# Gated attention's weighings in two column tiles of 64 queries, and the routers' products in column tiles

## The reference

```python
h = x @ rW1.T + rb1                       # 64 features
h = relu(layernorm(h) * ln_g + ln_b)
logits = h @ rW2.T + rb2                  # 8 experts
tp, ti = top_k(softmax(logits), 2)
...
def expert_step(acc, params):             # for each of the 8 experts
    q, k, v = x @ qw.T + qb_, x @ kw.T + kb_, x @ vw.T + vb_   # split into 16 heads of 8
    p = softmax(einsum('bhqd,bhkd->bhqk', q, k) * scale)
    o = einsum('bhqk,bhkd->bhqd', p, v)
    o = o.reshape(B, S, E) @ ow.T + ob_
    return (acc + o * g[..., None], None)
```

## Time and profile before

| | before |
|---|---|
| median of 3 runs | 3347.18 us |
| profiled execution, span | 3447.8 us |
| TensorE busy | 2817.4 us (82%) |
| VectorE busy | 1989.0 us (58%) |
| ScalarE busy | 1326.8 us (38%) |
| mean granted TensorE clock | 0.896 of full speed |

### The profile page before, as it was taken

One profiled execution on the slowest core, in us unless ns is written; L12 is line 12 of the kernel. 1 busy time (PEld: TensorE's weight loads), 2 busy tenths in 40 slices (PEclk: granted clock), 3 DMA queues, 4 the chain that ended last, 5 costly groups with the idle time before them and its releaser, 6 DMA issues.

```text
span 3447.8 us, 64821 instructions
## 1 busy us (share of the span) xinstructions
PE 2817.4 (82%) x24730; PEld 1996.0 (58%) x24818; DVE 1989.0 (58%) x6643; ACT 1326.8 (38%) x3062; POOL 635.1 (18%) x847
## 2 busy tenths in 40 slices
PE   5788988766687987988988988988988988987953
PEld 2344766634574864764764764755755755656743
DVE  2566444456544455666666666666766766765532
ACT  2343434433474743333333333334334334334521
POOL 0122112322312011121121121121111111111043
PEclk7888999877898998998998999998999999998977
DMA  7300647400373700000000000000000000003454
GB/s 254 113 23 22 199 129 208 131 19 22 125 229 99 240 23 7 3 9 7 3 9 7 3 9 7 3 9 7 3 9 7 3 9 4 3 4 112 130 168 147
DMA packets 146658, 217.14 MB, mean 63 GB/s; under 512 B 20392, under 2 KB 99248, under 8 KB 146224
## 3 DMA queue, kind: packets, MB, share of 16 engines
q1 hardware_dynamic: 134064, 187.80, 17.8%
q0 software_dynamic: 12288, 25.19, 2.4%
HBM read 159.83 MB, written 53.08 MB: 62 GB/s over the span
## 4 chain that ended last, share of the span: by engine, by line
PE 58%; DVE 21%; ACT 10%; issue 5%; another core or an unknown queue 2%; SPq 2%; DMA 1%; POOL 1%; DVEq 0%; POOLq 0%; ACTq 0%
PE bank L447 5%; PE bank L383 5%; ACT ex L1153 5%; PE bank L540 4%; PE bank L622 4%; DVE mx L1615 4%; PE bank L548 4%; PE bank L389 3%; PE bank L604 3%; PE bank L467 3%; PE bank L457 3%; PE bank L451 3%; PE bank L436 3%; PE bank L374 2%; PE bank L430 2%
## 5 line engine op out<-in xcount | busy, mean ns | idle before, releaser
L1153 ACT ACTIVATE ex<-bank 128x512 f32<-128x512 f32 x896 | 472.1, 600 | 692.7 <-PE bank L457 456.7
L1615 DVE TENSOR_REDUCE mx<-bank 128x4 bf16<-128x512 f32 x640 | 407.6, 684 | 133.2 <-PE bank L436 68.9
L965 POOL TENSOR_TENSOR rstd<-vare,power 128x2 f32<-128x2 f32 x192 | 136.1, 709 | 1377.9 <-DVE vare L1406 1377.9
L1032 POOL TENSOR_TENSOR oT<-oT 128x128 f32<-128x128 f32 x256 | 118.3, 462 | 916.2 <-DVE oT L1734 915.6
L540 PE MATMUL bank<-qm,expert 128*128 128x128 f32 x1872 | 260.2, 283 | 16.9 <-DMA expert<-in_moe 9.3
L974 POOL DMA_INDIRECT sent<-tail_tok,pos x192 | 192.0, 1000 | 394.0 <-DVE pos L1543 349.9
L383 PE MATMUL bank<-hT,wproj 128*128 128x256 f32 x736 | 242.8, 426 | 25.2 <-DVE oT L1734 8.5
L1607 DVE RECIPROCAL rden<-bank 128x16 f32<-128x16 f32 x160 | 41.1, 257 | 384.9 <-PE bank L476 347.1
L447 PE MATMUL bank<-qm,kf 32*128 32x512 f32 x1280 | 211.4, 723 | 57.1 <-ACT ex L1153 36.2
L540 PEld LDWEIGHTS bank<-qm,expert 128*128 128x128 f32 x1872 | 237.0, 198 | 28.6 <-DMA expert<-in_moe 15.5
L622 PEld LDWEIGHTS bank<-ev,ex 128*128 128x128 f32 x2048 | 247.6, 193 | 5.2 <-issue 0.4
(11 more groups left out here) (208 smaller groups left out, 5064.8 us busy)
## 6 DMA issues: line engine op xcount, KB each, us to landing
expert<-in_moe SPq DMA_DIRECT2D x78, 578.0 KB
expert<-in_moe SPq DMA_DIRECT2D x78, 512.0 KB
expert<-in_moe SPq DMA_DIRECT2D x78, 384.0 KB
sent<-zeros SPq DMA_DIRECT2D x8, 2560.0 KB, 12.8
ex<-sent SPq DMA_DIRECT2D x234, 64.0 KB
answered<-qm SPq DMA_DIRECT2D x234, 64.0 KB
ctxT<-ctx_kept SPq DMA_DIRECT2D x32, 128.0 KB
wproj<-in_wproj SPq DMA_DIRECT2D x1, 3072.0 KB
```

Of the source, the lines that this page charges most:

```text
L1153: give(nc.scalar.activation(ex[s][:, i], ps[:].rearrange("p (i q) -> p i q", i=4), ACT.Exp, scale=SCALE), *key)
L1615: give(nc.vector.tensor_reduce(mx[s][:, b, HB * i:HB * i + HB], ps[:].rearrange("p (i k) -> p i k", i=HB), AX.X, ALU.max), *k, "s", b, i)
```

## The change

`weigh` of the gated attention loads 64 of a block's 128 queries at a time. The first half's result goes to PSUM partitions 0 to 63, the second half's to 64 to 127, in the same columns of the bank as before. `by_token` gets a width: with `wide` under 128 the tokens are loaded in pieces of that many columns, and each piece's result goes to its own partitions. The routers use 32, the gated router's first product 64; values and outputs keep 128. Two costs that the planner reads are lowered by 0.9. What is read and written, and by which other engine, stays.

```diff
--- before.py
+++ after.py
@@ -383,11 +383,15 @@
                         mm = nc.tensor.matmul(ps[:, n * NT:(n + 1) * NT], W(weight), src[:], start=True, stop=True)
                     filled(mm, *k, what)
 
-                def by_token(k, what, weight, src, n, rows_=P):
+                def by_token(k, what, weight, src, n, rows_=P, wide=P):
+
+
                     ps = open_bank("g", *k, what)
                     for b in range(NB):
-                        mm = nc.tensor.matmul(ps[:, b * n:(b + 1) * n], src[0:rows_, seq(b)], weight,
-                                              start=True, stop=True)
+                        for at in range(0, P, wide):
+                            mm = nc.tensor.matmul(ps[at:at + wide, b * n:(b + 1) * n],
+                                                  src[0:rows_, b * P + at:b * P + at + wide], weight,
+                                                  start=True, stop=True)
                     filled(mm, *k, what)
 
                 def keys_values(k, key, value, rot=False):
@@ -402,7 +406,7 @@
                     if w.new("weights_in", 16 * n_loads):
                         pe.wait_ge(sem["weights_in"], 16 * n_loads)
                     taken(*t, "tT")
-                    by_token(t, "logits", router[:, ROUTERS[tail_layer(t[2])], :], attT[s], NE)
+                    by_token(t, "logits", router[:, ROUTERS[tail_layer(t[2])], :], attT[s], NE, wide=32)
 
                 def ranks(t):
 
@@ -619,16 +623,17 @@
                             ps = open_bank("g", *k, "o", p, b)
                             for c in range(4):
                                 j, i = c // 2, c % 2
-                                mm = nc.tensor.matmul(ps[:, c * (HE + 1):(c + 1) * (HE + 1)],
-                                                      ex[s][:, 2 * (p % 2) + i, 2 * b + j, :], ev[s][:, p % 2, b, i, :],
-                                                      start=True, stop=True)
+                                for part in range(2):
+                                    mm = nc.tensor.matmul(ps[head(part), c * (HE + 1):(c + 1) * (HE + 1)],
+                                                          ex[s][:, 2 * (p % 2) + i, 2 * b + j, head(part)],
+                                                          ev[s][:, p % 2, b, i, :], start=True, stop=True)
                             filled(mm, *k, "o", p, b)
 
                     def turn_mixed(p):
                         pe.wait_ge(sem[f"e_summed{s}"], w.next(f"e_summed{s}", NB))
                         turn(k, mixed[s][:, p % 2], f"mixedT{p}")
 
-                    by_token(k, "r", rw1[:], hT[s], HE)
+                    by_token(k, "r", rw1[:], hT[s], HE, wide=HE)
                     keys(0)
                     yield "router", 0.6, 3.0
                     keys(1)
@@ -639,7 +644,7 @@
                     keys(2)
                     yield "router", 0.6, 0.5
                     taken(*k, "rT")
-                    by_token(k, "logits", rw2[:], rT[s], NE, HE)
+                    by_token(k, "logits", rw2[:], rT[s], NE, HE, wide=32)
                     values(1)
                     yield "gate", 0.5, 4.0
                     pe.wait_ge(sem[f"slots_ready{s}"], w.next(f"slots_ready{s}"))
@@ -666,7 +671,7 @@
                             values(n)
                         if n >= 3:
                             turn_mixed(n - 3)
-                        yield "gated unit", 3.6 if 2 <= n < HP else 2.5 if n <= HP + 1 else 0.3, 0.3 if n <= HP else 1.5
+                        yield "gated unit", 2.7 if 2 <= n < HP else 1.6 if n <= HP + 1 else 0.3, 0.3 if n <= HP else 1.5
                     taken(*k, "wtsT")
                     if w.new("bias_in", 1):
                         pe.wait_ge(sem["bias_in"], 1)
```

## The result

The changed kernel takes 3343.35 us (median of 16 runs) where the kernel before takes 3351.30 on the same chip (16 runs). The ratio is 0.9975, 95% interval 0.9964 to 0.9987: 8 us faster, 4 to 12. I had forecast 59 us. The sign is right, the time lies in the range, and the size is out by a factor of seven.

What follows compares the result with a forecast made beforehand. TensorE was taken to bound the gated pass. Weighings 112.6, routers 15.7 + 5.2 + 3.5, less switches 61, gave 76 us; times 0.8, 61, scaled by 0.971 to 59, so 3288 us, range 3230 to 3365.

Steps and rivals of the forecast that it cites:

- rival C: All 128 weighings: column tiles load in turn, a round takes 0.112 us, switches are pure cost; 3383 us, chance 0.15.
- 68 forecast: All gated weighings: 0.88 us less each, minus 0.35 for switches, nets 0.53 us each, 68 us in all.
- the 0.145 and 0.20 of the forecast: TensorE's changes of tiling around a weighing: 0.145 us going in, 0.20 us coming out.
- 76 was forecast: TensorE work shed in the profiled execution: 112.6 + 15.7 + 5.2 + 3.5 - 61 = 76 us.
- 0.57 us or more on L383: Sign of the switch: the queries' two products before a weighing take 0.57 us or more, not 0.43.
- 54 + 57 = 111 ns: Round of a weighing by the skill's rule that loads overlap products only across row groups; equals the loads-in-turn time.
- How much reaches the end? … I take 0.8: Share of the 76 us of shed TensorE work that shortens the kernel: 0.8, so 61 us, scaled 59.
- 90 to 98% busy: TensorE's busy share in slices with weighings, from which shed work there was expected to shorten the pass.
- rival A: Only the weighing's part on the chain of waits counts: 0.56 x 76 = 43 us, scaled 41; 3306 us, chance 0.23.
- Rival B: Gated pass: TensorE's clock falls to 0.90, its work grows 58 us and gives the gain back; 3344 us, chance 0.10.
- I put the order at nothing, between -15 and +20 us: Planner's costs lowered by 0.9 us shift the two streams' steps in the pass; effect nothing, between -15 and +20 us.
- the likeliest case: The forecast itself for the whole kernel: 59 us faster, 3288 us, own range 3240 to 3310, chance 0.52.

Runs made afterwards that it cites:

- e0: The kernel before, unchanged, profiled once more: span 3429.94 us; its 14 timed runs on this chip have a median of 3434.39.
- e1: Changed kernel with the planner's costs of before (3.6 and 2.5), so tiles in the old order: 3396.64 us against 3434.39 for the kernel before, ratio 0.9887.
- e8: Kernel before with the maxima of the gated scores taken over half of the keys: 3346.55 us against 3349.55, ratio 0.9987.
- e9: e1's kernel with the maxima of the gated scores taken over half of the keys: 3311.09 us, ratio 0.9878 to the kernel before.
- e7: Changed kernel, both tiles, with planner's costs between old and new (3.1 and 2.0): 3398.20 us, ratio 0.9903 to the kernel before.
- e5: e1's kernel with the routers' products whole, so only the weighings in column tiles: 3415.10 us, ratio 0.9943 to the kernel before.
- e3: Kernel before without tiles, 8 of 16 loads of each gated weighing left out, 130 columns moved under each: 3385.01 us, ratio 0.9864.
- e11: e1's kernel with turn_mixed one unit later, ahead of the weighing: 3384.59 us against 3420.48 for the kernel before, ratio 0.9902.
- e12: Kernel before with turn_mixed one unit later, ahead of the weighing: 3459.54 us, ratio 1.0121, 41 us slower.
- e10: Kernel before with half of the weighings' products issued twice, 115 us of work added: 3405.12 us, ratio 1.0168, 56 us slower.
- e6: Kernel before with only the routers' products in column tiles, old costs: 3432.48 us, ratio 0.9990.
- e13: e1's kernel with three bf16 filler products in 48 places of plain attention, 31 us added: 3414.82 us, ratio 0.9986 to the kernel before.

## Why the prediction was off

**Right: what a weighing costs.** Two column tiles load side by side. In the changed kernel a round of two loads and two streams takes 0.058 us (0.057 forecast), and rival C, loads in turn, is out. A weighing with its two switches is 0.51 us shorter as a rule (0.53 forecast). Counted from the end of the product before each weighing to the end of the group behind it, all 128 take 281 us in e0 and 222 in e1, 59 less, and as much less from e8 to e9 (68 forecast). The switches, 0.15 us in and 0.14 out, are near the 0.145 and 0.20 of the forecast; a count of changes of tiling in the records of the two profiles, before and after, gives 345 more, where 338 was forecast. TensorE's busy time falls by 73 us in the gated pass (from 1743.34 to 1670.07) and by 82.5 in the whole profile (from 2793.3 to 2710.8), where 76 was forecast. One sign was misread: I looked for the switch as 0.57 us or more on L383 before the weighing. It stays 0.43, and the switch lies inside the weighing's 1.08. The "54 + 57 = 111 ns" under rival C should have used the stream's 55 ns, which gives 109 and changes nothing.

**Wrong, the larger step: "How much reaches the end? … I take 0.8".** About one half did in most pairs of kernels, less in one, and all of it in one. The work is an estimate from the rounds' and switches' times:

| run | work, us | time, us | share (95%) |
|---|---|---|---|
| e1 tiles, old order | -76 | -38 | 0.50 (0.37 to 0.66) |
| e7 tiles, costs in between | -76 | -33 | 0.44 (0.29 to 0.59) |
| e5 weighings' tiles alone | -59 | -20 | 0.33 (0.21 to 0.45) |
| e3 half the loads | -115 | -47 | 0.41 (0.31 to 0.50) |
| e9 against e8 | -76 | -36 | 0.47 (0.38 to 0.55) |
| e11 against e12 (late turn in both) | -76 | -75 | 0.99 (0.78 to 1.20) |
| e10 more products | +115 | +56 | 0.49 (0.45 to 0.53) |

Sums over the stretches of the gated pass show what became of it (plain: the eight long stretches without weighings; gated: all the rest, some gaps of about 21 us without weighings included; length and busy time of TensorE, us):

| | gated: length, busy, clock | plain: length, busy, clock |
|---|---|---|
| e0 before | 995, 926, 0.971 | 1015, 818, 0.911 |
| e1 tiles | 956, 855, 0.982 | 1028, 815, 0.908 |
| e3 half loads | 947, 833, 0.964 | 1022, 825, 0.903 |
| e6 routers' tiles alone | 997, 926, 0.971 | 1017, 809, 0.917 |
| e5 weighings' tiles alone | 960, 862, 0.974 | 1038, 835, 0.890 |
| e8 before, half maxima | 995, 934, 0.964 | 992, 811, 0.919 |
| e9 tiles, half maxima | 944, 854, 0.987 | 1022, 828, 0.889 |
| e10 more products | 1060, 1015, 0.995 | 995, 811, 0.911 |

From e0 to e1, TensorE sheds 71 us in the gated stretches and idles 32 more there (101 for 69); another 13 are lost in the plain ones, nearly all as idle time. From e8 to e9 the plain stretches lose 30, of which 17 are TensorE's own products at the lower clock, and from e6 to e5 they lose 21 with TensorE busy 26 us longer. I had read "90 to 98% busy" as bound by TensorE. But VectorE and ScalarE have to empty the banks that TensorE fills, and those copies kept their length and their place. When TensorE gets to a bank sooner it waits, as line 366 does. That wait is shown, with what ends it; that such waits are the whole of the loss is not shown, for no run took them away: half maxima (e9) left 11.8 of the 14.9 us at line 366, and the later turn moved them. This was rival A (0.56 of the work, 43 us in the profiled execution's time); its signs were that the weighing halves, the clock stays and the pass shrinks by 45 or less with more TensorE idle, and between e0 and e1 all of them came: 0.94 and 0.94, 26 us, 47 us more idle. I gave it 0.23. Rival B named the clock, too, but placed its fall over the whole pass (0.90). The pass kept 0.94, and where a fall shows (e5, e9), it is in the plain stretches.

**Wrong, the smaller step: "I put the order at nothing, between -15 and +20 us".** It costs 22 us (14 to 30), outside my bounds in the middle value. I saw what moved, stream 0's weighings against stream 1's output products, and asked only whether two TensorE-heavy ends in one period would collide. In the traces they don't cost: a period is as long as before. What costs is the shift itself, which one stream pays once and carries to the end of the pass.

**The sum again.** With the measured sizes: 76 us at 0.50 is 38, less 22 for the order is 16 us, each of the two known to some 10 us, so the measured 8 is no contradiction. A forecast with right sizes would have been about 3331. That the measured 3343.35 lies inside the stated range, 3230 to 3365, is luck: it is 33 us above the likeliest case's own 3240 to 3310 and 37 above A, whose mechanism came, since A had no cost for the order; it falls on B's 3344, whose mechanism did not come.

**What stays open.** Why the share is so often near one half, for less and for more work, when its parts differ from pair to pair: idle time, the clock of the plain stretches, or both. What a fifth bank in the ring, or an earlier copy of the queries, would bring: no run has either. Why a later turn costs the kernel before 41 us and the one with the tiles next to nothing, so that there the tiles pay in full. And what the routers' tiles bring. A kernel with the tiles, the old costs and nothing else (e1) is the fastest with the whole computation, 1.1% below the kernel before; e7 and e11 are its equals within the intervals.

## What to carry to other kernels

A high busy share says that an engine is worth relieving, not what the relief pays: measure that by a dose, adding a known amount of work at the same place (here 115 us made 56), before the change is priced. Less work need not mirror more work, and another order of steps can change the share (0.50 and 0.99 here), so look also at which buffer the relieved engine will want next and who has to empty it. When numbers feed a planner, change operations and numbers in two runs; here costs lowered by 0.9 us for steps that got 0.5 shorter lost over half of what the operations had won, and costs lowered by 0.5 lost nothing that shows (e7). And look at where streams stand to each other at the first and at the last period: an order can cost nothing in each period and still cost its shift once.

## What the runs showed of the hardware

- Two fp32 loads of 64 columns in two column tiles over all 128 rows run together with their streams: the loads of line 627 start about 7 and 51 ns apart in turn, 0.058 us a round of two, against 0.112 us for one load of 128 columns with its stream.
- A switch from full-array products into column tiles shows as 1.08 us for a weighing whose 16 rounds of 0.058 take 0.93, so 0.15; the switch back is 0.14 (L392 at 0.64 us against 0.50).
- More work can run faster: with 14.4 us more in a stretch of 126 us, TensorE's mean granted clock there went from 0.95 to 1.00 (e8 to e10), and less work can make products behind it slower, 2.02 us for 1.07 (e9). But work put in only for the clock did not pay (e13).
